# The order of a handful of steps in a Strassen-like FFN kernel: first pair, row sums, third product, weight sums

## The reference

```
x = x + 0.5 * ffn(layernorm(x))
x = x + ssm(layernorm(x))
x = x + 0.5 * ffn(layernorm(x))

ffn(x):  wu, wg, wd = ternary(W_up), ternary(W_gate), ternary(W_down)      # 512 -> 2048 -> 512
         hidden = silu(x @ wu.T) * (x @ wg.T)
         return hidden @ wd.T
ternary(w): scale = mean(|w|);  clip(round(w / scale), -1, 1) * scale
```

## Time and profile before

| | |
|---|---|
| median of 3 runs | 1861.08 us (1857.95 to 1861.36) |
| the profiled execution | 1857.95 us, span 1856.2 us |
| TensorE busy | 1775.1 us, 96% of the span |
| VectorE busy | 1376.1 us, 74% |
| ScalarE busy | 912.9 us, 49% |
| GpSimd busy | 822.5 us, 44% |
| mean granted TensorE clock | 0.999 |

### The profile page before, as it was taken

How to read it: one execution, slowest core, us unless ns; L and a number is a source line. 1 busy time by engine, 2 the same in 40 slices (tenths; PEclk the granted TensorE clock), 3 DMA queues, 4 the chain that set the end, 5 groups by cost and what they waited for, 6 DMA issues and landing times. The chain is left out here.

```text
span 1856.2 us, 35155 instructions
## 1 busy us (share of the span) xinstructions
PE 1775.1 (96%) x13078; PEld 1259.4 (68%) x13078; DVE 1376.1 (74%) x2311; ACT 912.9 (49%) x1372; POOL 822.5 (44%) x554
## 2 busy tenths in 40 slices
PE   5899999999999999999999999899999999999998
PEld 2374788888888854444444444454888888888887
DVE  6948787777865757697697696757777777877755
ACT  6314456474563645445444444425465474564643
POOL 0497253362442514454454454545253362443533
PEclk9999999999999999999999999999999999999999
DMA  7031121212214020111111111120211212112100
GB/s 317 1 92 33 54 41 46 74 31 65 40 45 137 0 97 21 60 35 51 57 40 51 57 34 35 58 68 20 67 41 46 64 35 71 40 45 62 40 23 23
DMA packets 132329, 102.79 MB, mean 55 GB/s; under 512 B 100752, under 2 KB 100752, under 8 KB 130448
## 3 DMA queue, kind: packets, MB, share of 16 engines
q1 hardware_dynamic: 132240, 101.77, 18.1%
HBM read 49.59 MB, written 25.17 MB: 40 GB/s over the span
## 5 line engine op out<-in xcount | busy, mean ns | idle before, releaser
L445 POOL TENSOR_TENSOR f_hlo<-f_h,f_hhi 128x768 f16<-128x768 f32 x135 | 201.7, 1494 | 626.6 <-ACT f_hhi L591 598.3
L1036 PE MATMUL f_down_ps<-wd,f_hhi 128*128 128x256 fp8e4 x1440 | 317.7, 273 | 2.5 <-DVE xa L793 1.7
L1036 PE MATMUL f_down_ps<-wd,f_hlo 128*128 128x256 fp8e4 x1440 | 317.7, 273 | 0.0
L1110 PE MATMUL f_gate_ps<-spare 128*128 128x256 f16 x2496 | 306.2, 272 | 0.0
L1110 PEld LDWEIGHTS f_gate_ps<-spare 128*128 128x128 fp8e4 x2496 | 236.7, 97 | 40.7 <-issue 0.5
L1110 PE MATMUL f_up_ps<-spare,wu 128*128 128x256 f16 x1664 | 212.2, 272 | 6.8 <-ACT f_gate_ps L640 6.5
L793 DVE SCALAR_TENSOR_TENSOR xa<-f_down_ps,out_scale,xa 128x512 f32<-128x512 f32 x195 | 136.3, 743 | 63.4 <-PE f_down_ps L1036 63.2
L1110 PEld LDWEIGHTS f_up_ps<-spare,wu 128*128 128x128 fp8e4 x1664 | 159.1, 98 | 32.2 <-issue 10.1
L1036 PEld LDWEIGHTS f_down_ps<-wd,f_hhi 128*128 128x128 f16 x1440 | 140.9, 98 | 20.6 <-issue 4.2
L1036 PEld LDWEIGHTS f_down_ps<-wd,f_hlo 128*128 128x128 f16 x1440 | 140.8, 98 | 16.2
L445 POOL TENSOR_TENSOR f_hlo<-late,f_hhi 128x1024 f16<-128x1024 f32 x68 | 148.3, 2181 | 4.1 <-ACT f_hhi L597 4.1
(11 more groups left out here) (223 smaller groups left out, 3381.7 us busy)
## 6 DMA issues: line engine op xcount, KB each, us to landing
res<-xa SPq DMA_DIRECT2D x16, 1024.0 KB, 4.3
xa<-res SPq DMA_DIRECT2D x16, 1024.0 KB, 5.6
xa<-in_u SPq DMA_DIRECT2D x8, 1024.0 KB, 5.5
xa<-res SPq DMA_DIRECT2D x32, 256.0 KB, 2.7
res<-xa SPq DMA_DIRECT2D x32, 256.0 KB, 2.0
spare<-in_w_up SPq DMA_DIRECT2D x4, 1024.0 KB, 10.6
late<-in_w_gate SPq DMA_DIRECT2D x4, 1024.0 KB, 17.9
late<-in_w_in SPq DMA_DIRECT2D x1, 2320.0 KB, 8.7
```

What stands on the lines that cost most here:

```text
L445: last = nc.gpsimd.tensor_tensor(hlo[:, p, a:b, :], src, hhi[:, p, a:b, :], ALU.subtract)
L1036: last = nc.tensor.matmul(at, part[:, p, kind, m * P:(m + 1) * P], wd[:, weight, p, :], start=(p == 0 and part is hhi and (m == 0 or name ...
L1110: last = nc.tensor.matmul(acc[:, j * HT:(j + 1) * HT], w[:, k, e * P:(e + 1) * P], xop[part][:, o, k, :, :], start=(fresh and (j, k, part) ...
```

## The change

Seven edits of order:

1. The first pair of a `seven` group on TensorE goes P1, P5, P2, P6, P1 of the next pair, P7, P3, P5 of the next, P4, P2 of the next, where it went P1, P1 of the next, P2, P5, P6, P5 of the next, P7, P3, P4, P2 of the next. ScalarE's `copy_p5` of the first pair follows `copy_p1` directly.
2. Half 0 of P3's last pair comes before half 1's pairs 0 to 6, where it came after them.
3. `variance` and `inv_std` of a `seven` group move from pair 5 to pair 6.
4. In `group`, `stats`, `variance`, `inv_std` and the rows' steps come one to two steps i later; the last `rows_low` falls on i = 14.
5. GpSimd forms seven weight sums before group 1 and nine in and after it, where it formed ten and six.
6. The last group is written out on TensorE and not a turn of the loop; its P5 waits for no rows. VectorE's extra count of `rl_done` goes.
7. The sixteen transposes at the end of f1 move into the last group's down projection, two sets ahead of P5 and two ahead of P6.

The numbering of the products that these orders change (`product_at`) is left out of the diff.

```diff
...
@@ -466,7 +463,7 @@
                                              (S2, S1, A11, ALU.subtract), (S4, A12, S2, ALU.subtract))[which]
                             nc.gpsimd.tensor_tensor(dst, a, b, op, saturate=False).then_inc(s_done, 1)
 
-                        S_EARLY = 10
+                        S_EARLY = 7
 
                         def direct_group():
                             for p in range(HK):
@@ -486,20 +483,23 @@
 
                         def group(g):
                             for p in range(HK):
-                                if p == 2:
+                                if p == 3:
                                     inv_std(g + 1)
                                 low_parts(g, p, 0, sums[0])
                                 low_parts(g, p, 1, sums[0])
                                 if p == HK - 1:
                                     inv_std(g + 2)
-                                if first and S_EARLY + p < 16:
+                                if first:
                                     s_sum(S_EARLY + p)
+                            if first:
+                                for i in range(S_EARLY + HK, 16):
+                                    s_sum(i)
 
                         def seven(g, ln):
                             for p in range(HK):
                                 low_parts(g, p, 0, sums[p % 2])
                                 low_parts(g, p, 1, sums[p % 2])
-                                if p == 5 and ln is not None:
+                                if p == 6 and ln is not None:
                                     inv_std(ln)
 
                         if first:
@@ -612,8 +612,8 @@
                                 if i and i % 2 == 0:
                                     hid_high(g, i // 2 - 1)
                                     sums_high(g, i // 2 - 1)
-                                if i in (7, 11):
-                                    rows_high(g + 1, (i - 7) // 4)
+                                if i in (9, 13):
+                                    rows_high(g + 1, (i - 9) // 4)
                             hid_high(g, HK - 1)
                             sums_high(g, HK - 1)
                             for c in range(2):
@@ -653,10 +653,9 @@
 
                         def seven(g):
                             copy_p1(g, 0)
+                            copy_p5(g, 0)
                             for p in range(HK):
                                 up_first(g, p)
-                                if p == 0:
-                                    copy_p5(g, 0)
                                 copy_u2(g, p)
                                 if p:
                                     hid_high(g, p - 1)
@@ -805,9 +804,6 @@
                                 elif ln is not None and ln < NG:
                                     for do, c in STEPS_OF.get(name, ()):
                                         do(ln, c)
-                            if g == NG - 2:
-
-                                dve.sem_inc(rl_done, 2)
 
                         def direct_group(between):
                             for i in range(KE):
@@ -837,17 +833,17 @@
                                 hidden(g, i)
                                 if i % 2:
                                     pair_sums(dve, nc.vector, g, i // 2)
-                                if i in (1, 2):
-                                    stats(g + 1, 2 * i - 2)
-                                    stats(g + 1, 2 * i - 1)
-                                if i == 3:
+                                if i in (2, 3):
+                                    stats(g + 1, 2 * i - 4)
+                                    stats(g + 1, 2 * i - 3)
+                                if i == 5:
                                     variance(g + 1)
-                                if i in (5, 9):
-                                    rows_start(g + 1, (i - 5) // 4)
-                                if i in (6, 10):
-                                    rows_sums(g + 1, (i - 6) // 4)
+                                if i in (7, 11):
+                                    rows_start(g + 1, (i - 7) // 4)
                                 if i in (8, 12):
-                                    rows_low(g + 1, (i - 8) // 4)
+                                    rows_sums(g + 1, (i - 8) // 4)
+                                if i in (10, 14):
+                                    rows_low(g + 1, (i - 10) // 4)
                                 if i in (13, 14):
                                     stats(g + 2, 2 * i - 26)
                                     stats(g + 2, 2 * i - 25)
@@ -891,7 +887,7 @@
                                 if ln is not None and p in (3, 4):
                                     stats(ln, 2 * p - 6)
                                     stats(ln, 2 * p - 5)
-                                if ln is not None and p == 5:
+                                if ln is not None and p == 6:
                                     variance(ln)
                                 hidden_second(g, p)
                                 hidden_first(g, p)
@@ -1013,6 +1009,7 @@
                             weight, kind, _ = PRODUCT[name]
                             j = ORDER.index(name)
                             if m == 0 and p0 == 0:
+
                                 if BANK[j] == 2:
 
                                     pe.wait_ge(sil_done, after(KE * (g + 1) - 1))
@@ -1034,24 +1031,24 @@
                             for p in range(p0, p1):
                                 for part in (hhi, hlo):
                                     last = nc.tensor.matmul(at, part[:, p, kind, m * P:(m + 1) * P], wd[:, weight, p, :],
-                                                            start=(p == 0 and part is hhi and (m == 0 or name != "P3")),
-                                                            stop=(p == HK - 1 and part is hlo), skip_group_check=(name == "P3"))
-                            if m == 1 and p1 == HK:
+                                                            start=(p == 0 and part is hhi),
+                                                            stop=(p == HK - 1 and part is hlo))
+                            if m == 1:
                                 last.then_inc(down_done, 1)
 
-                        def down(g, filled):
+                        def down(g, filled, leave):
 
                             product(g, "P2", 0, filled, HK - 1)
                             product(g, "P1", 0, 0, HK - 1)
                             product(g, "P3", 0, 0, HK - 1)
-                            for name in ORDER[0:2]:
+                            for name in ORDER[0:3]:
                                 product(g, name, 0, HK - 1, HK)
                                 product(g, name, 1)
-
-                            product(g, "P3", 1, 0, HK - 1)
-                            for m in range(2):
-                                product(g, "P3", m, HK - 1, HK)
                             for name in ORDER[3:]:
+                                if leave and name in ("P5", "P6"):
+                                    k = 0 if name == "P5" else 2
+                                    transposes(1, k)
+                                    transposes(1, k + 1)
                                 product(g, name, 0)
                                 product(g, name, 1)
 
@@ -1094,7 +1091,7 @@
                         def group(g):
                             for i in range(KE):
                                 up_gate(g, i)
-                            down(g, 0)
+                            down(g, 0, False)
 
 
                         SEVEN = dict(P1=(wu[:, 0:2, :], 0), P2=(wu[:, 2:4, :], 1), P3=(ws[:, 3, :, :], 4), P4=(wg[:, 2:4, :], 6),
@@ -1126,8 +1123,8 @@
                             pe.wait_ge(u1_done, after(pair_of(g, p) + 1))
                             of_pair(p, "P2", A_ps[p % 2], False).then_inc(p_done, 1)
 
-                        def p5(g, p):
-                            if p == 0:
+                        def p5(g, p, rows_too):
+                            if p == 0 and rows_too:
 
                                 pe.wait_ge(rl_done, after(2 * (g - NC) + 4))
                             pe.wait_ge(c5_done, after(pair_of(g, p)))
@@ -1149,30 +1146,27 @@
                             pe.wait_ge(c22_done, after(pair_of(g, p) + 1))
                             of_pair(p, "P4", C_ps, False).then_inc(p_done, 1)
 
-                        def seven(g):
+                        def seven(g, rows_too, leave):
                             FILL = 4
                             if first:
                                 pe.wait_ge(s_done, 16)
                             p1(g, 0)
-                            p1(g, 1)
+                            p5(g, 0, rows_too)
                             p2(g, 0)
-                            p5(g, 0)
                             for p in range(HK):
                                 p6(g, p)
```

(19 more changed lines are left out.)

11 lines of the change are left out of this document (4 added, 7 removed).

## The result

| | before | changed | ratio, 95% interval |
|---|---|---|---|
| median of 4 runs each, first chip | 1861.16 us | 1881.38 us | 1.0104 [1.0083, 1.0125] |
| same kernels again, second chip | 1859.05 | 1876.75 | 1.0095 [1.0078, 1.0112] |
| and on a third | 1860.90 | 1878.64 | 1.0100 [1.0084, 1.0115] |
| profiled execution (first chip) | 1857.95 | 1870.56 | |

On the first chip the changed kernel ran seven times, profiled execution included, between 1870.56 and 1882.08 us; the median of the seven is 1880.66.

A forecast was written before the change was run, and what follows sets the result against it. TensorE, busy 96% of the span, was taken as the bound. Terms 1.4 + 6.4 + 2.9 + 0.5 + 0.3 = 11.5 us gave 1869.5 from the profiled 1857.95, or 1872.6 from the median; forecast 1871, range 1861 to 1879.

The forecast's parts named there:

- The step that failed: Edit 6, TensorE's written-out last group: its straight code was costed at 0, at most 1 us in all.
- 13 x 0.50: Edit 1: P2's wait for ScalarE's copy of P1 goes in thirteen `seven` groups, gaining 6.5 us.
- the new wait: Edit 1: first pair's P5 waits 0.72 us for `rows_low` in eleven groups, losing 7.9 us.
- The 0.26 + 0.26 us: Edit 3: P2's last pair and P3 each lose 0.26 us in ten groups with a variance, 0.52 together.
- waits hidden: Rival, chance 0.18 for small loss or nothing: L348 slips ahead, signals partly hidden, direct groups come out even; 1865 to 1862.
- The 0.41 of the other three groups: Edit 2: P3's last pair waits 0.41 us for GpSimd's last low part in three groups without a variance.
- the term of 2.9: Edit 4, tail of group 0 of f2: `rows_low` between the last `hidden` delays the group's end by 2.9 us.
- the long wait: Edits 4 and 5, group 1 of f1: TensorE's 2.81 us wait for `hidden` comes again, at i = 14.
- the early part: Edits 4 and 5, group 1 of f1: wins about 1.5 us, then lost by the tail; net +0.5 us.
- faster (the stall goes): Rival, chance 0.07: direct groups' stall in group 1 of f1 goes, 4.4 us, and copies' 6.5 us; about 1850.
- The 1/sqrt: Rival, chance 0.03: `inv_std` behind pair 6 holds VectorE 1.00 us, lengthening P3's wait in ten groups; 1880.
- the larger ones: Rivals of larger loss: direct groups' new stalls with lower clock and tails, 1877, chance 0.10; 1/sqrt hold, 1880, chance 0.03.

The follow-up runs named there:

- b_first2: The kernel before with edit 1 alone (P5 of the first pair second): 1858.72 us, ratio 0.9989.
- b_p3var2: The kernel before with edits 2 and 3 alone (P3's half 0 closed first, variance and inv_std one pair later): 1866.86 us, ratio 1.0039.
- b_direct2: The kernel before with edits 4 and 5 alone (rows' steps later in direct groups, seven early weight sums): 1863.95 us, ratio 1.0025.
- a_loop2: The changed kernel without edits 6 and 7, so the last group stays in the loop: 1869.69 us, ratio 1.0053 against the kernel before.
- b_unroll_2nd: The kernel before with only the last group of each FFN written out behind the loop: 1867.94 us, ratio 1.0044.
- after_third: The changed kernel again, unchanged, beside the version without edit 7 on the same chip: 1878.64 us.
- a_unroll: The changed kernel without edit 7, so edits 1 to 6 with the transposes behind the last group: 1876.65 us.
- d_left_sum: `d_left` with the weight sum behind pair 3 of group 1 of f1 left out there and later ones moved on: 1846.72 us, ratio 0.9927.
- d_left: The kernel before with P5 of the next pair covering the copy, and the previous group's last 16 matmuls between P1 and P2: 1848.54 us; again (`d_left_2nd`), 1846.93.
- b_leave2: The kernel before with edits 6 and 7 alone (last group written out, transposes between its products): 1871.83 us, ratio 1.0071.
- after_again: The changed kernel once more, unchanged, for spread and another profile: its profiled execution took 1880.15 us.

## Why the prediction was wrong, step by step

| step | forecast | measured |
|---|---|---|
| edit 1 | +1.4 | -2.3 (`b_first2`) |
| edits 2 and 3 | +6.4 | +5.9 (`b_p3var2`); +6.2 by the groups' lengths |
| edits 4 and 5 | +3.4 | +4.9 (`b_direct2`); +4.4 by the two groups' lengths |
| edits 1 to 5 | +11.2 | +8.7 (`a_loop2`) |
| edit 6, written out | 0 to +1 | +7.0 alone (`b_unroll_2nd`) and with edits 1 to 5 |
| edit 7 | +0.3 | +0.2 to +0.5 by lengths; +2.0 by medians (`after_third` less `a_unroll`) |
| all, by medians | +10 | +17.7, +17.7, +20.2 |

**The step that failed** is "Writing out the last group adds straight code; the groups before the loop are straight code and have no gap, so I cost it at 0, at most 1 us in all". What the runs showed in its place is +7.0 us for that edit alone: TensorE waits up to 2.5 us for pieces of the copy's code, and some of these waits are followed by the lower clock. The groups before the loop were a wrong witness. Most of their matmuls have 512 columns and take 0.22 us; those of a `seven` group 0.109. The first turn of the loop, also new code, would have been a nearer one, and it takes 0.2 to 0.6 us more than the later turns. Neither shows the 1.3 to 10.3 us of the copy behind the loop; the bound should have been left open at the top. That the pace of the matmuls is the reason isn't shown: the first turn has the same pace, and so have the copies' down projections, where no piece is waited for by more than 0.4 us.

**Edit 1** was right in both waits and their counts, and wrong in its sign. The term mis-sized is 13 x 0.50, "Gain: 13 x 0.50 = 6.5 us": from start to start the wait cost 0.66, and the pauses beside it, put at nothing, 0.24, so 13 x 0.90 = 11.7 us; the new wait cost 11 x 0.82 = 9.0, where 7.9 were counted.

**Edits 2 and 3** held in the sum by luck. The 0.26 + 0.26 us of the ten groups with a variance came as 0.48 + 0: P2's wait was mis-sized, and P3's there did not come, since L348 slipped ahead. That is the condition which the prediction gave to its lower end of 3.4 us and to the rival *waits hidden*, and it held without their small loss. The 0.41 of the other three groups held. **Edit 4** held in its wait; its size is 2.5 us, and 3.0 with the lower clock behind that wait, which the term of 2.9 didn't have. **Edits 4 and 5 in group 1**: the long wait came again one pair later, 2.82 us, but the early part won nothing and the tail lost 1.0, not 2; in the kernel before its cause is the sum of weights behind pair 3, as `d_left_sum` shows by taking it away. **The rivals**: faster (the stall goes) is refuted, and `d_left_sum` shows that the stall's shrinking to 0.81 us is worth 0.6 to 1.5 us in group 1's length, and not the 4.4 counted, since the tail gives the rest back. The 1/sqrt does not hold the pair sums (`b_p3var2`). None of the larger ones named the code.

**The range** ended at 1879, 2.4 us short of the first median, and held the other two. That was luck: errors of 2.5 us down (edits 1 to 5) and 9 to 11 us up (edits 6 and 7) set each other off in part.

**Still open**: why the fetch of a piece starts ahead of need in one execution and only at the place itself in another, so that a written-out group costs 1.3 us in one place and 10.3 in another, and the same one of the changed kernel 2.2 in one execution and 6.5 in another (52.6 and 56.9, where the same group in the loop takes 50.4); and why it starts early enough in the loop's first turn. The code's position, moved once by 64 instructions, moved the places of the waits and not their sum.

## What to carry to other kernels

A loop's last turn taken out of the loop to save a wait is not free: here TensorE reached the end of the code that it had before the next piece had come. Count the bytes of new code per engine, look for issue waits beside packets of the instruction queue, and keep one body for all turns. Size a wait from start to start of the instructions around it, against the same pair of instructions unhindered, not from the idle time shown, and add the pauses that are too short to be shown. And where a wait must be covered, moving work across the loop's edge (`d_left`) gave 12 to 14 us where a change of order inside gave 2.

## What the runs showed of the hardware

TensorE's code comes in pieces of 16 KB, and in second code behind a loop it waits up to 2.5 us for one, with the DMA engines otherwise idle. The places are fixed, some 120 matmuls with their loads apart, and 64 instructions ahead of them move them by 30 or 31 matmuls; whether TensorE waits at one, and how long, changes from one execution to the next. The packet takes 0.9 to 1.5 us in either case: the wait is long where it starts late. The Trainium skill, "Runtime: NRT & Kernel Launch", section "Instruction fetch mechanics", says that the next block is fetched while the current one executes and that the cost of crossing a 16 KiB boundary is mostly hidden. In the loop's first turn the trace agrees (0.2 to 0.6 us); in the copy behind the loop it differs, with 1.3 to 10.3 us a group, and by that sentence edit 6 would have cost next to nothing, as I had it.

A wait of 2 us or so makes the lower clock possible but doesn't decide it. The waits of 2.40 and 2.52 us in `b_leave2` were followed by it and made 1.7 us dearer, that of 1.99 us in `after_again` too; that of 2.48 us in the same group was not, nor was the one of 2.82 us at 175.32 in the changed kernel's first profile (eight matmuls in 1.89 us), while that of 2.81 us in the earlier trace rows was. The same wait of the same kernel goes either way: 2.81 us at 168 us, in `d_left` without the lower clock behind it and in `d_left_2nd` with it. Five such times in one execution and one in another of the same kernel are a good part of its spread.
